# A graph attention layer with a state-space block: GpSimd's preamble products in pieces of 256 columns in place of 1024

## The reference

```python
x = x + gnn(layernorm(x), h0, a, temp, adj)          # x: 4096 x 128, adj: 4096 x 4096 of 0 and 1
x = x + mamba2(layernorm(x), W_in, conv_w, ...)      # 32 chunks of 128 rows, one after the other

def gnn(x, h0, a, temp, adj):
    e = leaky_relu(x @ a[:128] + (x @ a[128:]).T, 0.2)
    U = softmax(where(adj > 0, e, -9e15), axis=1)
    rowsum = sum(U * 0.5 * U, axis=1)
    feat = mix_1(x, U @ x, x * rowsum)               # then a soft threshold of 1e-6
    return mix_2(feat, U @ feat, rowsum, h0)
```

## Time and profile before

| | |
|---|---|
| time, median of 3 runs | 782.66 us (782.0 to 783.86) |
| the profiled execution | 781.77 us, of which the span of the core is 780.0 us |
| TensorE busy | 737.7 us (95%) |
| VectorE busy | 726.2 us (93%) |
| ScalarE busy | 670.5 us (86%) |
| GpSimd busy | 628.5 us (81%) |
| mean granted clock of TensorE | 0.991 |

### The profile page before, as it was taken

One profiled execution on the slowest core, in us unless ns is written; L12 is line 12 of the kernel. 1 busy time (PEld: TensorE's weight loads), 2 busy tenths in 40 slices (PEclk: granted clock), 3 DMA queues, 4 the chain that ended last, 5 costly groups with the idle time before them and its releaser, 6 DMA issues.

```text
span 780.0 us, 21076 instructions
## 1 busy us (share of the span) xinstructions
PE 737.7 (95%) x6049; PEld 707.6 (91%) x6049; DVE 726.2 (93%) x1898; ACT 670.5 (86%) x1428; POOL 628.5 (81%) x1215
## 2 busy tenths in 40 slices
PE   3679999999999999988899999999999999999987
PEld 1369999999999999987899999999999999999976
DVE  6999999999999999897999999999999999999986
ACT  5999898989899898976898989898989898989864
POOL 5584888888888888887888888888888888888863
PEclk9999999999999999999999999999999999999999
DMA  7689898989898986023121212121212121210000
GB/s 219 187 250 319 299 291 280 336 253 348 263 326 280 316 284 257 24 50 96 41 72 43 71 42 72 40 71 40 71 40 71 40 71 40 71 42 18 10 4 15
DMA packets 97962, 110.43 MB, mean 142 GB/s; under 512 B 6866, under 2 KB 89714, under 8 KB 97906
## 3 DMA queue, kind: packets, MB, share of 16 engines
q1 hardware_dynamic: 97906, 109.78, 43.5%
HBM read 90.87 MB, written 18.89 MB: 141 GB/s over the span
## 4 chain that ended last, share of the span: by engine, by line
PE 63%; DVE 22%; issue 6%; POOL 5%; ACT 3%; DVEq 1%; DMA 0%; ACTq 0%; POOLq 0%
PE accA L1708 21%; PE accC L1717 21%; DVE code L777 9%; DVE maskC L785 4%; PE ps L1818 3%; PE ps L1802 2%; PE ps L1835 2%; PE ps L1816 2%; PE ps L1820 2%; PE ps L1647 2%; PE ps L1854 2%; PE ps L1800 2%; PE ps L1827 1%; PE ps L1837 1%; PE ps L1843 1%
## 5 line engine op out<-in xcount | busy, mean ns | idle before, releaser
L1345 ACT ACTIVATE maskA<-code 128x1024 fp32r<-128x1024 int8 x256 | 269.2, 1054 | 20.5 <-DVE code L777 19.8
L1708 PE MATMUL accA<-Y,maskA 128*128 128x260 f32 (+1 forms) x1792 | 264.3, 290 | 1.6 <-ACT maskA L1345 1.2
L1717 PE MATMUL accC<-Y,maskC 128*128 128x260 f32 (+1 forms) x1792 | 253.4, 284 | 2.8 <-DVE maskC L785 2.7
L1708 PEld LDWEIGHTS accA<-Y,maskA 128*128 128x128 f32 x1792 | 231.5, 189 | 4.6 <-issue 2.3
L1717 PEld LDWEIGHTS accC<-Y,maskC 128*128 128x128 f32 x1792 | 229.2, 190 | 3.7 <-DVE maskC L785 3.6
L785 DVE TENSOR_SCALAR maskC<-code 128x1024 fp32r<-128x1024 int8 x256 | 206.6, 808 | 0.3
L777 DVE SCALAR_TENSOR_TENSOR code<-f_rows,neg_f,ps 128x512 int8<-128x512 int8 (+1 forms) x256 | 178.0, 738 | 0.3 <-DVE neg_f L741 0.2
L1282 ACT ACTIVATE edges<-adj_in 128x1024 int8<-128x1024 f32 x128 | 135.6, 1061 | 1.6 <-DMA adj_in<-in_adj_dram 1.6
L638 POOL TENSOR_TENSOR room_r<-room,room_r 128x256 fp32r<-128x256 f32 x128 | 97.7, 791 | 2.5
L1070 DVE SCALAR_TENSOR_TENSOR room<-room 128x128 f32<-128x128 f32 x270 | 86.3, 341 | 0.0
L1647 PE MATMUL ps<-ident,edges 128*128 128x128 bf16 x512 | 42.5, 223 | 12.0 <-ACT edges L1282 11.9
(11 more groups left out here) (275 smaller groups left out, 1622.2 us busy)
## 6 DMA issues: line engine op xcount, KB each, us to landing
adj_in<-in_adj_dram SPq DMA_DIRECT2D x128, 512.0 KB, 5.1
edge_codes<-code SPq DMA_DIRECT2D x32, 512.0 KB, 5.6
code<-edge_codes SPq DMA_DIRECT2D x32, 512.0 KB, 3.3
xn<-in_x_dram SPq DMA_DIRECT2D x4, 512.0 KB, 5.7
room<-in_x_dram SPq DMA_DIRECT2D x32, 64.0 KB, 1.8
room<-in_L_gnn_h_dram SPq DMA_DIRECT2D x32, 64.0 KB, 1.9
out_dram<-room SPq DMA_DIRECT2D x32, 64.0 KB, 1.6
room<-in_L_ffn_W_in_dram SPq DMA_DIRECT2D x1, 192.0 KB, 2.5
```

Source lines behind the costliest of these rows:

```text
L1345: s.activation(maskA[:, b % MASKS], src, ACT.Relu, bias=1.0 - LINK, scale=-1.0).then_inc(S["maskA_ready"], 1)
L1708: t_.matmul(accA[k][:, 0:2 * cols], maskA[:, b % MASKS, l * P:(l + 1) * P], y2_of(jt, 0) if cols == F else Y[:, jt, 0, :, 0:cols], start=j ...
L1717: m = t_.matmul(accC[k][:, 0:2 * cols], maskC[:, b % MASKS, l * P:(l + 1) * P], y2_of(jt, 1) if cols == F else Y[:, jt, 1, :, 0:cols], sta ...
```

## The change

GpSimd's eight products and four low parts of 1024 columns are each issued as four instructions of 256 columns (two tiles) one behind the other. The waits stand before the first of the four, and the semaphore is raised by the last. No other engine's program is changed.

```diff
-                g.tensor_tensor(y_first(q, side), xn[:, q * JB:(q + 1) * JB, :],
-                                colw[:, side, q * JB:(q + 1) * JB, 0:1].broadcast_to([P, JB, F]), ALU.mult).then_inc(S[prod], 1)
+                for at in range(0, JB, 2):
+                    m = g.tensor_tensor(y_first(q, side)[:, at:at + 2], xn[:, q * JB + at:q * JB + at + 2, :],
+                                        colw[:, side, q * JB + at:q * JB + at + 2, 0:1].broadcast_to([P, 2, F]), ALU.mult)
+                m.then_inc(S[prod], 1)
 
             def y_low_c(q):
                 pool.wait_ge(S["yC_hi"], q + 1)
-                g.tensor_tensor(Y[:, q * JB:(q + 1) * JB, 1, 1, 0:F], y_first(q, 1),
-                                Y[:, q * JB:(q + 1) * JB, 1, 0, 0:F].bitcast(F32), ALU.subtract).then_inc(S["yC_done"], 1)
+                for at in range(0, JB, 2):
+                    two = slice(q * JB + at, q * JB + at + 2)
+                    m = g.tensor_tensor(Y[:, two, 1, 1, 0:F], y_first(q, 1)[:, at:at + 2], Y[:, two, 1, 0, 0:F].bitcast(F32), ALU.subtract)
+                m.then_inc(S["yC_done"], 1)
```

## The result

The changed kernel takes 786.08 us (median of 20 runs, 784.67 to 787.73), the one before in the same comparison 782.79 us. The ratio is 1.0040, with a 95% interval of 1.0031 to 1.0048: 3.3 us slower. Forecast were 785.7, and 3.0 slower. The profiled execution has a span of 783.6 us, 3.6 more than before.

The account below looks back on a forecast made before the run. VectorE was taken to bound the stretch where the changed lines run, TensorE's products from 61.2 us. A 2.1 us delay plus 0.9 for the clock made 3.0, giving 785.7 us on the base of 782.66; range 782.6 to 787.3.

Parts of the forecast that it names:

- VectorE's gain: Between 27.7 and 57.8 us VectorE waits for a piece, not a whole GpSimd instruction: about 4.2 us gained on VectorE.
- TensorE doesn't hang on VectorE: From 53.3 to 61.2 us only the C products wait for a mask: VectorE's gain is worth at most 0.3 us directly.
- The 0.66 us of ScalarE: L875's gain lets ScalarE start its column copy 0.66 us sooner, then work without a pause until the load at 50.33.
- GpSimd's price: A product piece costs 0.575 us, a low-part piece 0.70; the eight products and four low parts add 5.4 us on GpSimd.
- Who waits: ScalarE's casts wait for GpSimd's products, group four's first 2.4 us late; the last sign and TensorE follow, C products 2.1 late.
- VectorE waits for GpSimd's last low part at 61 to 63 us: GpSimd's last low part ends at 63.3 instead of 57.84, so VectorE's next mask comes 2.2 us late.
- the two agree: TensorE's C products 2.1 us late and VectorE's next mask 2.2 us late were said to match.
- The clock: TensorE's pause from about 51.2 to 55.7 us may halve its clock: up to 1.7 us late, 0.9 taken.
- VectorE would absorb part of it: Early VectorE, as full as TensorE in 61 to 95 us, absorbs part of the clock's delay; half, 0.9 us, was taken.
- 0.54 us a piece or less: Rival: cheaper GpSimd pieces, slack hides most of them; +0.7 us at 0.54, nothing at 0.52; 782.7 to 783.4; chance 0.18.
- The rival of the other side: Shorter waits win at L875 and at 61.19 with pieces under 0.52 us: 0.95 us gained, 781.7; chance 0.06.
- cutting alone gives no more than 0.95 us: Even free cutting of GpSimd's instructions gains at most 0.95 us, as TensorE's chain from 53.3 us hangs on ScalarE.

Follow-up runs that it names:

- Filling the pause: 12 additional matmuls on TensorE between turns 14 and 15 of the changed kernel: ratio 1.0014, again 1.0024, to the kernel before; with 24 matmuls 1.0036.
- 512 columns: All twelve GpSimd instructions in two pieces of 512 columns each, against the kernel before: 781.07 us, ratio 0.9985.
- low parts only: Only the four low parts cut into four pieces of 256 columns, products whole, against the kernel before: 781.46 us, ratio 0.9982.

## Why the prediction was right, point by point

The mechanism was the forecast one, and the time lay 0.4 us from it. The terms, from the profile after:

1. *VectorE's gain.* L875 under 0.6: 0.49. Masks 1.2 and 1.3: 1.10 and 1.22. Right. The low parts of side A gained 0.95 us (6.79 to 5.84 for the four) where 0.2 was forecast, so the whole was 5.4 us and not 4.2. Of it only the 0.33 us of waiting at 61.19 reached TensorE.
2. *TensorE doesn't hang on VectorE.* Right: VectorE stood 2.31 and 4.49 us waiting for TensorE. The 0.66 us of ScalarE were forecast as kept until the 15th load. They weren't: its cast at 33.46 waited 0.80 for the second product, and its cast at 44.95 stands 0.2 behind the one before, not 0.66 ahead. This step was missed; the waits that the forecast named began only at 45 us.
3. *GpSimd's price.* 0.575 and 0.70 us a piece forecast; 4.60/8 and 2.82/4, 0.575 and 0.705, measured. The estimate worked out from the Trainium skill (GPSIMD Engine Reference, section 3.1), 0.66 for a low piece, was too low; the trace's row decided rightly.
4. *Who waits.* The first product of group three was in time (cast at 44.95, without a wait); forecast was a wait until 45.5. The second was cast at 47.22, 0.56 late, forecast 1.1. The first of group four at 53.25, 1.95 late, forecast 2.4. TensorE's turn at 55.31, forecast 55.7. Each of these is 0.4 to 0.5 too late in the forecast, as it let the first product of group three be ready at 45.5 where it was at 44.9. Part of that is its price for meeting VectorE: GpSimd was to lose 2.0 us more to it up to there (1.1, 0.6 and 0.3), and by the rows it lost 1.45 more (1.05, 0.45 and 1.40 against 0.99 and 0.46 before). Less the 0.33 us of waiting at 61.19, this term is 1.64 us where 2.1 was forecast.
5. *VectorE waits for GpSimd's last low part at 61 to 63 us.* This was wrong. That part ended at 62.0 and not at 63.3, and VectorE waited for TensorE's sums at that time, until 63.13. The forecast put all 5.4 us on top of the old end, 57.84. But GpSimd had stood 2.58 us idle ahead of that part, and the added work fills this first. Its "the two agree" rested on an end that was 1.3 us too late.
6. *The clock.* Forecast 0.9, half of what a full fall costs. From 55.31 to 64.40 are 9.09 us where from 53.34 to 61.19 less 0.33 were 7.52: 1.57 us, nearly all of the 1.7. Filling the pause gave 1.3 and 2.3 us at C2 against the two profiles of the change, and 2.0 us in the times of the same chip. The reasoning that VectorE would absorb part of it failed: VectorE was early, but TensorE was full from 61 us on, and nothing absorbed a delay of TensorE there.

The sum was 2.1 + 0.9; measured 1.64 + 1.57 = 3.21 at C2. Two sizes were off by -0.5 and +0.7 and cancelled: the path was forecast, but that the time came within 0.4 us was in part luck.

As for the rivals: 0.54 us a piece or less was excluded by the rows. The rival of the other side was real for another size of piece: with 512 columns the shorter waits win, by 1.2 us. That cutting alone gives no more than 0.95 us is in keeping with C2, which came 0.96 us sooner with 512 columns and 0.75 with low parts only. The times don't decide it: 0.15 and 0.18% are 1.2 and 1.4 us, with intervals from 0.2 and 0.3 us up to over 2.

## What to carry to other kernels

Cutting an engine's instruction so that a neighbour waits less has a price per piece and a gain that falls off with each halving: the two masks took 2.39 and 2.86 us with whole instructions of GpSimd, 1.53 and 1.53 with two pieces, 1.10 and 1.22 with four. Count the slack of every product up to its reader, and cut only as finely as the slack pays: here two pieces, not four. Before a wait on one engine is shortened, look which engine's chain starts the next stage; VectorE was given back some 5 us here and had nothing to do with them. An instruction that stands behind a wait without needing it (here the sign) can go ahead of it. That took most of the loss away, but only as far as the sign's own input, a load, was there.

## What the runs showed of the hardware

- GpSimd's cost of an extra instruction was 0.14 to 0.15 us: for products by two widths (0.575 x 4 against 1.86), for low parts by three (2.50 and 2.82 against 2.36).
- TensorE's granted clock fell to 0.50, that is 1.2 GHz, around the last turn in three of the fourteen profiles. The pause ahead of the turn was 2.94, 1.60 and 3.66 us there, and the 16 sums took 3.32, 3.67 and 3.78 us, where at 2.4 GHz they took 1.95 to 2.05. In other profiles pauses of 1.47, 1.50, 1.75 and 2.65 us at the same place left them at 2.05, so the length of this pause alone doesn't decide it. The Trainium skill (TensorE: Matmul & The Clock Gate, section on HAM oscillation) says that waits between bursts do this. The three falls agree, the four pauses without one show that not every such wait does it. Twelve idle matmuls in the pause of the change (2.90 us) took the fall away in both profiles and made the kernel 2.0 us faster.
- VectorE, let in between two pieces, cost GpSimd about the time of VectorE's own instruction. Among the first eight products, the piece at 31.84 took 1.59 us where an undisturbed one takes 0.61, while VectorE's low part ran (31.49 to 32.96); the eight took 5.65 us, eight undisturbed 4.60.
